# Experts' first layer with the weights as the loaded operand: its rows come out turned, without transposes and copies

## The chip, the cores and the metric

The kernel runs on one core of a Trainium2 chip. The metric is the time of one execution on the device in microseconds (us), smaller being better. The time of before is the median of three runs. Beside it stands one profiled execution, from which all rows come.

## The reference, cut to what matters

Eight images of 64 channels x 128 x 128 go through a normalisation, two 1x1 convolutions and a residual. The pixels then become tokens (16384 per image, 64 values each). Of every image each of 32 experts takes the 8 tokens with the highest gate value, pools them into one row, passes the row through two layers, and adds the result, weighted, back to its 8 tokens:

```
pooled = jnp.einsum('bked,bke->bed', gathered, topv)        # b=8 images, k=8, e=32 experts, d=64
h = jnp.concatenate([pooled.transpose(1, 0, 2), ones], axis=-1)
h = jax.nn.gelu(jnp.einsum('ebd,edh->ebh', h, weight1), approximate=False)   # d=65, h=256
h = jnp.concatenate([h, ones], axis=-1)
out = jnp.einsum('ebh,eho->ebo', h, weight2)                # o=64
outputs = outputs.at[jnp.arange(Bn)[:, None], flat_idx].add(weighted)
```

The change concerns the first of the two expert layers, and the way from it to the second.

## The kernel before

All is written by hand: each engine has its own instruction stream and runs it in order, and semaphores tie the streams together. The eight images go through a pipeline of 8 x 8 steps that fills the first 565 us. Behind it comes a tail in which the experts run, in two passes over the images: `PASSES` is images 0 to 5 (pass 0) and 6 to 7 (pass 1).

The tail's stream on TensorE (PE) is, for pass 0: pool the gathered tokens (`experts_in`, L573), the first layer (`experts_up`, L606), two spreads of a statistic over the partitions for image 7 (`spread_stat` "E", L485), turn the hidden rows (`experts_turn`, L616), one spread for the merge of image 7's candidates ("M", L473), the second layer (`experts_down`, L626), the rows of the outputs (`expert_rows`, L635), and the sums of what is added to the tokens (`add_rows`, L650). Pass 1 is `experts_in`, `experts_up`, `add_rows(1)` (second half of pass 0's sums), `spread_pixels(3)` (L582), `experts_turn`, `experts_down`, `expert_rows`, and two more `add_rows`.

In the first layer the loaded operand of a matmul is the pooled rows (65 values of 32 columns, of which 8 are one expert's images; the others are not used), and the weights stream past it, 256 columns for each expert. Four experts stand side by side in the array, in four groups of 32 columns. The hidden rows come out with (slot of 32, image) on the partitions and the hidden index along the row, in four PSUM banks; ScalarE (ACT) applies the gelu to 128x512 at a time (`gelu`, L835), TensorE transposes 16 blocks of 128x128, and VectorE (DVE) copies the used columns out of PSUM into `ht` (`turned`, L1178). The second layer reads `ht`. Every matmul in float32 stands in the trace as two instructions, each with a weight load of its own; a transpose is one.

DVE's stream in pass 0 goes through the top values and places of image 7 (L963, L968), two scalings of its logits that need the two spreads (`use_spread` "E", L869), the four copies of `turned(0)`, and `candidates(7)` (L975 to L981), whose last instruction waits for ACT's exponentials (L745) and releases the "M" spread.

Of the kernel before, what the change touches and what calls it, by code (L numbers as in the profile page):

```python
# [9 lines left out]
ACT = mybir.ActivationFunctionType  # L10
AX = mybir.AxisListType

P = 128
C = 64
HALVES = 2
NB = 8
PIX = 128 * 128
HW = PIX // HALVES
CH = 512
SUB = 256  # L20
# [5 lines left out]
HID = 256  # L26
# [4 lines left out]
PASSES = ((0, 6), (6, 8))  # L31
# [68 lines left out]
def mk_metaformer_kernel(nc, x, gn_w, gn_b, w1T, b1, w2T, b2, gateT, gate_b, e_w1, e_w2, e_b2, *outs):  # L100
    ctx = ExitStack()
    with ctx:
        def sb(name, shape, dt=F32):
            return ctx.enter_context(nc.sbuf_tensor(name, shape, dt))

        def banks(name, n=1):
            return ctx.enter_context(nc.psum_tensor(name, [P, n * CH], F32))

        def sem(name):
            return ctx.enter_context(nc.semaphore(name))  # L110
# [3 lines left out]
        us = [sb(f"us{i}", [P, HW]) for i in range(2)]  # L114
# [8 lines left out]
        ident = sb("ident", [P, P])  # L123
# [62 lines left out]
        ew1 = us[0][0:C + 1, :].rearrange("d (e n) -> d e n", e=NE)  # L186
        ew2 = xs[0][:, 0:NE * 2 * C].rearrange("p (e k o) -> p e k o", e=NE, k=2)
# [3 lines left out]
        pool_f = late[0:C + 1, 0:NE * NB + 3 * NB]  # L191
        zsq = [eq[:, 6:8].rearrange("p b f i -> p (b f i)"), late[:, CH:2 * CH]]
        diags = [eq[:, 7 - p % 2].rearrange("p f i -> p (f i)") for p in range(3)] + [late[:, 2 * CH:3 * CH]]
        hg = us[1][:, 0:4 * CH]
        ht = us[1][:, 4 * CH:5 * CH]
        eot = us[1][:, 5 * CH:7 * CH]
        zc = us[1][:, 7 * CH:9 * CH].rearrange("p (b g c) -> p b g c", b=NB, g=GATHERS)
# [5 lines left out]
        tl, st1, st2 = banks("tl", 2), banks("st1"), banks("st2")  # L203
        lgp, pt = tl[:, 0:CH], tl[:, CH:2 * CH]
        first_banks = [bc, cv]
        bc_of = [bc[:, 0:CH], bc[:, CH:2 * CH]]
        pc, pd = cv[:, 0:CH], cv[:, CH:2 * CH]
# [1 line left out]
        gnb_p = bc[:, 2:3]  # L209
        mrg_p = bc[:, CH:CH + 4 * MRG]  # L210

        h_banks, add_banks = (st1[:], pt, pd, pc), (lgp, st2[:])


        w_in, x_in = sem("w_in"), [sem(f"x_in{m}") for m in range(NG)]
# [16 lines left out]
        idx_out = sem("idx_out")  # L232
        rows_in = [sem("rows_in0"), sem("rows_in1")]
        scattered = [sem(f"scattered{i}") for i in range(len(outs))]
        zero_ready, ht_ready = sem("zero_ready"), sem("ht_ready")
        t2_done = sem("t2_done")
        ln_steps, rvar_ready, rln_done, ry_ready = (sem(n) for n in ("ln_steps", "rvar_ready", "rln_done", "ry_ready"))
        z_ready, pool_done, pooled_ready = (sem(n) for n in ("z_ready", "pool_done", "pooled_ready"))
        ew_in, l1_done, gelu_done, l2_done = (sem(n) for n in ("ew_in", "l1_done", "gelu_done", "l2_done"))
# [21 lines left out]
        def place(b, i):  # L261

            return PIECE * ((PIECES * b + i) % RING)

        def piece(b, i):
            return lg[:, place(b, i):place(b, i) + PIECE]

        def used(eng, it, kind, k):

            eng.wait_ge(bc_used, job_count(it, kind, k))  # L270
# [86 lines left out]
        def _(pe):  # L357
# [219 lines left out]
            def spread_pixels(p):  # L577

                pe.wait_ge(diag_ready, p + 1)
                pe.wait_ge(bc_used, job_count(7, "L", 1) if p == 0 else job_count(7, "L", 3) if p < 3 else job_count(8, "M", 7))  # L580
                wait(pe, eq_ready, p - 1)
                pe.matmul(bc_of[p % 2], ones[:], diags[p], start=True, stop=True).then_inc(pxr_done, 1)  # L582
# [15 lines left out]
            def experts_up(p):  # L598

                pe.wait_ge(pooled_ready, p + 1)  # L600
                if p == 0:
                    pe.wait_ge(ebias_ready, 1)
                    pe.wait_ge(tok_done, NU * NB)
                for e in range(NE):
                    grp, slot = e // 4, e % 4
                    mm = pe.matmul(h_banks[grp // 2][32 * slot:32 * slot + 32, HID * (grp % 2):HID * (grp % 2) + HID],  # L606
                                   pool_f[:, NB * e:NB * e + 32], ew1[:, e, :], start=True, stop=True, skip_group_check=True)
                    if e % 8 == 7:
                        mm.then_inc(l1_done, 1)

            def experts_turn(p):

                for i in range(4):
                    pe.wait_ge(gelu_done, 4 * p + i + 1)
                    for k in range(4):
                        mm = pe.transpose(h_banks[i][:, P * k:P * k + P], hg[:, CH * i + P * k:CH * i + P * k + P], ident[:])  # L616
                    mm.then_inc(t2_done, 1)

            def experts_down(p):

                pe.wait_ge(ht_ready, 4 * p + 4)
                for e in range(0, NE, 2):
                    for k in range(2):
                        for par in range(2):
                            col = 32 * (2 * (e // 4) + k) + NB * ((e + par) % 4)
                            mm = pe.matmul(pd[C * par:C * par + C, NB * (e // 2):NB * (e // 2) + NB], ew2[:, e + par, k, :],  # L626
                                           ht[:, col:col + NB], start=(k == 0), stop=(k == 1), skip_group_check=True)
                mm.then_inc(l2_done, 1)

            def expert_rows(p):  # L630
# [27 lines left out]
            for h in range(HALVES):  # L658
                mm = pe.matmul(pd[C * h:C * h + C, 0:NE], eb2, ident[0:NE, 0:NE], start=True, stop=True)
# [3 lines left out]
            experts_up(0)  # L663
            for k in (2, 3):
                spread_stat(NB, "E", k)
            experts_turn(0)
            spread_stat(NB, "M", NB - 1)
            experts_down(0)
            expert_rows(0)
# [2 lines left out]
            experts_up(1)  # L672
            add_rows(1)
            spread_pixels(3)
            experts_turn(1)
            experts_down(1)
            expert_rows(1)
            for i in (2, 3):
# [4 lines left out]
        def _(act):  # L683
# [146 lines left out]
            def gelu(p):  # L830

                nc.scalar.preload_act_table_set("gelu_and_others")
                for i in range(4):
                    act.wait_ge(l1_done, 4 * p + i + 1)
                    nc.scalar.activation(hg[:, CH * i:CH * i + CH], h_banks[i], ACT.Gelu).then_inc(gelu_done, 1)  # L835

            gelu(0)
            nc.scalar.preload_act_table_set("natural_log_exp_and_others")
# [8 lines left out]
        def _(dve):  # L847
# [117 lines left out]
            def top_places(t, i):  # L965

                link = Steps(dve, top_steps, TOP_STEPS * t + 2 * i + 1)
                link(nc.vector.max_index(top_i[:, K * i:K * i + K], cnd[:, K * i:K * i + K], piece(t, i)))  # L968
                nc.vector.tensor_scalar(nmax[:, i:i + 1], cnd[:, K * i:K * i + 1], -1.0, None, ALU.mult).then_inc(top_ready, 1)

            def candidates(t):

                link = Steps(dve, top_steps, TOP_STEPS * t + 2 * PIECES)
                pix = cnd[:, CAND:2 * CAND]
                link(nc.vector.tensor_scalar(top_hi[:], top_i[:], 0xFFFFFF00, None, ALU.bitwise_and))  # L975
                link(nc.vector.scalar_tensor_tensor(out=pix, in0=top_i[:], scalar=rowoff[:], in1=top_hi[:],
                                                    op0=ALU.add, op1=ALU.add))
                link(nc.vector.tensor_tensor(pix, pix, pixbase[:], ALU.add))
                assert link.n + 2 * PIECES == TOP_STEPS, link.n
                dve.wait_ge(expl_done, PIECES * (t + 1))  # L980
                nc.vector.tensor_tensor(cnd4[:], cnd[:].unsqueeze(1).broadcast_to([P, 4, MRG]),  # L981
                                        kmask[:].unsqueeze(2).broadcast_to([P, 4, MRG]), ALU.mult).then_inc(cnd4_ready, 1)
# [116 lines left out]
            def equal_pixels(p):  # L1099

                dve.wait_ge(pxr_done, p + 1)
                for i, b in enumerate((2 * p, 2 * p + 1)):
                    for f in range(GATHERS):
                        ins = nc.vector.tensor_scalar(eq[:, b, f, :], bc_of[p % 2][:, SUB * i:SUB * i + SUB],
                                                      px_all[:, b, f:f + 1], None, ALU.is_equal)
                ins.then_inc(eq_ready, 1)
                dve.wait_ge(eq_ready, p + 1)
# [18 lines left out]
            for q in range(4):  # L1126
                r = slice(32 * q, 32 * q + 32)
# [35 lines left out]
            def pooled(p):  # L1163

                b0, b1 = PASSES[p]
                dve.wait_ge(pool_done, p + 1)
                if p == 0:
                    dve.wait_ge(zero_ready, 1)
                else:
                    dve.wait_ge(l1_done, 4)  # L1170
                nc.vector.tensor_copy(pool_f[0:C, 0:NE * NB].rearrange("c (e b) -> c b e", b=NB)[:, b0:b1],
                                      pc[0:C, 0:NE * NB].rearrange("c (b e) -> c b e", b=NB)[:, b0:b1]).then_inc(pooled_ready, 1)

            def turned(p):

                for i in range(4):
                    dve.wait_ge(t2_done, 4 * p + i + 1)
                    nc.vector.tensor_copy(ht[:, P * i:P * i + P].rearrange("p (a b) -> p a b", b=NB),  # L1178
                                          h_banks[i].rearrange("p (a r) -> p a r", r=32)[:, :, 0:NB]).then_inc(ht_ready, 1)

            def expert_outs(p):

# [39 lines left out]
            for i in (2, 3):  # L1222
                top_values(7, i)
                top_places(7, i)
            turned(0)
            candidates(7)
            lns(nc.vector.tensor_tensor(id2[:], ident[:, 0:C], ident[:, C:P], ALU.add))
            use_spread(NB, "M", NB - 1)
# [7 lines left out]
            result_rows(0)  # L1236
            result_rows(1)
            equal_pixels(3)
            turned(1)
            expert_outs(1)  # L1240
            contributions(1)
            for i in (2, 3):
# [101 lines left out]
```

## Time and profile before

| what | value |
|---|---|
| median of three runs | 655.95 us (655.65 to 656.5) |
| profiled execution, its own time | 656.33 us |
| span of the profiled execution | 654.6 us, 14326 instructions |
| busy share of PE / PE weight loads / DVE / ACT / POOL | 84 / 43 / 75 / 66 / 29 % |
| mean granted clock of TensorE | 0.918 |

The profile counts TensorE's matmuls (PE) and its weight loads (PEld) apart. "Granted clock" is the share of full speed: 1.00 is 2.4 GHz, 0.50 is 1.2 GHz. Times are counted from the start of the span.

### The profile page before, as it was taken

How to read it: one execution, taken by the hardware profiler on the slowest of the kernel's cores; microseconds unless marked ns; L12 is line 12 of the kernel's file. 1: busy time of each engine (PE TensorE's matmuls, PEld its weight loads, DVE VectorE, ACT ScalarE, POOL GpSimd, SP SyncE). 2: the span in 40 equal slices, each digit the busy share in tenths (PEclk: the TensorE clock that was granted, in tenths of full speed). 3: DMA queues.
4: the chain of work that ended last, by engine and by line, in shares of the span. 5: the costliest groups of instructions: out<-in, count | busy, mean ns of one | idle time of the engine just before them, and what ended most of it. 6: DMA issues, size and time to landing. Idle time of an engine off the chain costs nothing.

```text
span 654.6 us, 14326 instructions
## 1 busy us (share of the span) xinstructions
PE 547.3 (84%) x5838; PEld 282.9 (43%) x5838; DVE 488.5 (75%) x955; ACT 428.9 (66%) x603; POOL 186.9 (29%) x110
## 2 busy tenths in 40 slices
PE   3659999998989898989898989898979888576983
PEld 1333444444444344435443544354434333346673
DVE  5574565789888988898889888988887779695221
ACT  2454778678967896789678967896779556361200
POOL 1008252116220622062206120612052451101332
PEclk9955999999999999999999999999989989975565
DMA  8950246533653364336533643364111555300000
GB/s 198 198 124 6 85 133 173 154 95 100 182 141 98 106 180 136 101 105 175 139 105 106 177 132 107 111 170 131 67 64 67 159 155 157 109 2 6 12 14 8
DMA packets 26753, 73.40 MB, mean 112 GB/s; under 512 B 4152, under 2 KB 4152, under 8 KB 22592
## 3 DMA queue, kind: packets, MB, share of 16 engines
q1 hardware_dynamic: 25664, 71.44, 39.7%
q0 software_dynamic: 1024, 1.05, 0.6%
q8 instruction: 46, 0.75, 0.5%
q14 instruction: 19, 0.16, 0.1%
HBM read 38.40 MB, written 34.08 MB: 111 GB/s over the span
## 4 chain that ended last, share of the span: by engine, by line
PE 43%; DVE 30%; ACT 13%; issue 11%; DMA 2%; POOL 0%; SPq 0%; ACTq 0%; DVEq 0%; POOLq 0%
PE st L364 11%; ACT junk L740 7%; DVE xs L881 7%; PE cv L375 6%; PE cv L383 6%; PE tl L392 5%; PE bc L485 5%; DVE us L871 4%; DVE lg L869 3%; PE cv L626 2%; DVE top_i L968 2%; ACT tok L705 2%; DVE us L873 2%; PE tl L401 2%; ACT hid L700 2%
## 5 line engine op out<-in xcount | busy, mean ns | idle before, releaser
L1285 POOL TENSOR_TENSOR xs<-xs,us 128x1024 f32<-128x1024 f32 x64 | 151.2, 2380 | 366.3 <-DVE xs L881 173.1
L881 DVE SCALAR_TENSOR_TENSOR xs<-cv,vecs,xs 128x1024 f32<-128x1024 f32 x64 | 82.0, 1282 | 47.7 <-PE cv L383 47.6
L733 ACT ACTIVATE sqc<-us 128x1024 f32<-128x1024 f32 x64 | 67.5, 1054 | 45.4 <-DVE us L871 44.6
L700 ACT ACTIVATE hid<-cv,b1n 128x1024 f32<-128x1024 f32 x64 | 71.3, 1114 | 36.8 <-PE cv L375 36.3
L871 DVE TENSOR_TENSOR us<-xs,bc 128x1024 f32<-128x1024 f32 x60 | 72.9, 1215 | 19.6 <-PE bc L485 19.2
L392 PEld LDWEIGHTS tl<-ident,xs 128*128 128x128 f32 x512 | 63.8, 195 | 53.5 <-issue 53.3
L364 PE MATMUL st<-xs,stat_w 128*32 128x256 f32 x1024 | 74.4, 412 | 10.0 <-DMA xs<-in_x 8.9
L740 ACT ACTIVATE junk<-us 128x1024 bf16<-128x1024 f32 x64 | 67.3, 1051 | 22.8 <-DVE gsum L873 22.2
L873 DVE CUSTOM_DVE_ANT_0 us<-us,bc 128x1024 f32<-128x1024 f32 x60 | 72.9, 1215 | 11.2 <-PE bc L485 9.9
L485 PE MATMUL bc<-rstd_s,spread 32*128 32x256 f32 x368 | 47.7, 336 | 35.6 <-DVE gsum L873 20.3
L392 PE MATMUL tl<-ident,xs 128*128 128x128 f32 x512 | 76.4, 294 | 0.8 <-ACT lg L715 0.8
L375 PE MATMUL cv<-us,w1n 64*64 64x512 f32 x512 | 72.0, 633 | 2.5 <-DVE b1n L936 1.9
L383 PE MATMUL cv<-hid,w2bd 64*64 64x512 f32 x512 | 70.6, 622 | 2.8 <-ACT hid L700 2.8
L401 PE MATMUL tl<-xs,gcen 128*32 128x256 f32 x1024 | 69.4, 389 | 4.0 <-ACT tok L705 4.0
L720 ACT ACTIVATE sqx<-xs 128x1024 f32<-128x1024 f32 x64 | 67.0, 1047 | 1.0 <-PE st L364 0.8
L485 PEld LDWEIGHTS bc<-rstd_s,spread 32*128 32x128 f32 x368 | 28.9, 192 | 86.1 <-DVE gsum L873 42.3
L705 ACT ACTIVATE tok<-tl 128x1024 f32<-128x1024 f32 x64 | 65.0, 1016 | 1.2 <-PE tl L392 1.2
L715 ACT ACTIVATE lg<-tl 128x512 f32<-128x512 f32 x64 | 37.8, 590 | 34.7 <-PE tl L401 31.9
L485 PE MATMUL bc<-mean_s,spread 32*128 32x256 f32 x240 | 31.8, 342 | 19.5 <-DVE us L871 15.1
L364 PEld LDWEIGHTS st<-xs,stat_w 128*32 128x32 f32 x1024 | 31.3, 116 | 33.6 <-issue 13.6
L401 PEld LDWEIGHTS tl<-xs,gcen 128*32 128x32 f32 x1024 | 27.1, 110 | 34.4 <-issue 11.3
L869 DVE TENSOR_TENSOR lg<-lg,bc 128x1024 f32<-128x1024 f32 x32 | 38.9, 1214 | 1.6 <-PE bc L485 1.3
(184 smaller groups left out, 664.6 us busy)
## 6 DMA issues: line engine op xcount, KB each, us to landing
xs<-in_x SPq DMA_DIRECT2D x64, 512.0 KB, 6.8
out_rows<-tok SPq DMA_DIRECT2D x64, 512.0 KB
us<-in_e_w SPq DMA_DIRECT2D x8, 260.0 KB
xs<-in_e_w SPq DMA_DIRECT2D x8, 256.0 KB
sqc<-out_rows,idx_all POOLq DMA_INDIRECT x16
out_rows<-sqc,idx_all POOLq DMA_INDIRECT x16, 2.1
vecs<-in_b SPq DMA_DIRECT2D x4, 0.2 KB, 13.6
gate_bias<-in_gate_b SPq DMA_DIRECT2D x4, 0.1 KB, 11.9
```

The source lines that it names most:

```text
L364: mm = pe.matmul(dst[32 * c:32 * c + 32], stat_w[:, q, :], src[:, col:col + SUB], start=first and m == 0 and sub == 0, stop=True, skip_gro ...
L375: mm = pe.matmul(cv[C * sl:C * sl + C, CH * h:CH * h + CH], w1n[par][r, r], half_chunk(us[par], u, h, sl), start=True, stop=True)
L383: mm = pe.matmul(cv[C * h:C * h + C, CH * sl:CH * sl + CH], w2bd[r, r], hid[r, CH * h:CH * h + CH], start=True, stop=True)
L392: mm = pe.transpose(tl[:, P * k:P * k + P], unit(xs[par], u)[:, k:UN:8], ident[:])
L401: mm = pe.matmul(lgp[NE * c:NE * c + NE, SUB * sl:SUB * sl + SUB], gcen[:, NE * h:NE * h + NE], xs[par][:, col:col + SUB], start=True, sto ...
L485: mm = pe.matmul(out[:, CH * sl + SUB * i:CH * sl + SUB * i + SUB], weights, stat[32 * c:32 * c + 32, :], start=True, stop=True)
L700: nc.scalar.activation(hid[:], cv[:], ACT.Relu, bias=b1n[:, par:par + 1]).then_inc(h_done, 1)
L740: nc.scalar.activation(junk[:], unit(us[n % 2], k), ACT.Square, accum_out=gsq[:, k:k + 1]).then_inc(usq_done, 1)
L871: ins = nc.vector.tensor_tensor(unit(us[n % 2], k), unit(xs[n % 2], k), stat[:], ALU.subtract)
L873: ins = nc.vector.tensor_tensor_reduce(unit(us[n % 2], k), unit(us[n % 2], k), stat[:], 1.0, 0.0, ALU.mult, ALU.add, gsum[:, k:k + 1])
L881: nc.vector.scalar_tensor_tensor(out=xu, in0=cv[:], scalar=vecs[:, 3:4], in1=xu, op0=ALU.add, op1=ALU.add).then_inc(x1_done, 1)
L1285: nc.gpsimd.tensor_tensor(xu, xu, su, ALU.add).then_inc(s_done, 1)
```

## The change

The first layer swaps its operands. For each expert and each half of its 256 hidden values, a 65x128 block of the weights is loaded, and the pooled rows of the pass (6 columns in pass 0, 2 in pass 1) stream past. The hidden values come out on the partitions, which is what the second layer reads; so the transposes on TensorE, the copies on DVE and their two semaphores go. The gelu writes straight into `ht`, in two instructions a pass instead of four. The second layer takes only the pass's columns (6 or 2 instead of 8), and its wait is on the gelu, once for each half of the experts.

```diff
-        h_banks, add_banks = (st1[:], pt, pd, pc), (lgp, st2[:])
+        h_banks, add_banks = (st1, pc), (lgp, st2[:])
...
+        def place_of(e, k):
+
+            return NB * (2 * e + k)
...
+                b0, b1 = PASSES[p]
                 for e in range(NE):
-                    grp, slot = e // 4, e % 4
-                    mm = pe.matmul(h_banks[grp // 2][32 * slot:32 * slot + 32, HID * (grp % 2):HID * (grp % 2) + HID],
-                                   pool_f[:, NB * e:NB * e + 32], ew1[:, e, :], start=True, stop=True, skip_group_check=True)
-                    if e % 8 == 7:
+                    for k in range(2):
+                        col = place_of(e, k)
+                        mm = pe.matmul(h_banks[e // 16][:, col % SUB + b0:col % SUB + b1], ew1[:, e, P * k:P * k + P], pool_f[:, NB * e + b0:NB * e + b1],
+                                       start=True, stop=True)
+                    if e % 16 == 15:
                         mm.then_inc(l1_done, 1)
 
-            def experts_turn(p):
-
-                for i in range(4):
-                    pe.wait_ge(gelu_done, 4 * p + i + 1)
-                    for k in range(4):
-                        mm = pe.transpose(h_banks[i][:, P * k:P * k + P], hg[:, CH * i + P * k:CH * i + P * k + P], ident[:])
-                    mm.then_inc(t2_done, 1)
-
             def experts_down(p):
 
-                pe.wait_ge(ht_ready, 4 * p + 4)
+                b0, b1 = PASSES[p]
                 for e in range(0, NE, 2):
+                    if e % 16 == 0:
+                        pe.wait_ge(gelu_done, 2 * p + e // 16 + 1)
                     for k in range(2):
                         for par in range(2):
-                            col = 32 * (2 * (e // 4) + k) + NB * ((e + par) % 4)
-                            mm = pe.matmul(pd[C * par:C * par + C, NB * (e // 2):NB * (e // 2) + NB], ew2[:, e + par, k, :],
-                                           ht[:, col:col + NB], start=(k == 0), stop=(k == 1), skip_group_check=True)
+                            col, out = place_of(e + par, k), NB * (e // 2)
+                            mm = pe.matmul(pd[C * par:C * par + C, out + b0:out + b1], ew2[:, e + par, k, :],
+                                           ht[:, col + b0:col + b1], start=(k == 0), stop=(k == 1), skip_group_check=True)
...
-            experts_turn(0)
...
-            experts_turn(1)
...
-                for i in range(4):
-                    act.wait_ge(l1_done, 4 * p + i + 1)
-                    nc.scalar.activation(hg[:, CH * i:CH * i + CH], h_banks[i], ACT.Gelu).then_inc(gelu_done, 1)
+                b0, b1 = PASSES[p]
+                for i in range(2):
+                    act.wait_ge(l1_done, 2 * p + i + 1)
+                    half, h = (t.rearrange("p (a b) -> p a b", b=NB)[:, :, b0:b1]
+                               for t in (ht[:, SUB * i:SUB * i + SUB], h_banks[i][:, 0:SUB]))
+                    nc.scalar.activation(half, h, ACT.Gelu).then_inc(gelu_done, 1)
...
-            def turned(p):
-
-                for i in range(4):
-                    dve.wait_ge(t2_done, 4 * p + i + 1)
-                    nc.vector.tensor_copy(ht[:, P * i:P * i + P].rearrange("p (a b) -> p a b", b=NB),
-                                          h_banks[i].rearrange("p (a r) -> p a r", r=32)[:, :, 0:NB]).then_inc(ht_ready, 1)
```

TensorE's stream in pass 0, from the first layer (L606) to the second (L626), before; a row's last figures are the output's shape and the number of matmuls in the source:

```order
L606 MATMUL st<-us,lg 32x256 x8
L606 MATMUL tl<-us,lg 32x256 x8
L606 MATMUL cv<-us,lg 32x256 x16
L485 MATMUL bc<-rstd_s,spread 128x256 x8
L616 MATMUL st<-ident,us 128x128 x4
L616 MATMUL tl<-ident,us 128x128 x4
L616 MATMUL cv<-ident,us 128x128 x8
L473 MATMUL bc<-cnd,fold 128x272
L626 MATMUL cv<-us,xs 64x8 x64
```

The same place now, where the first layer is L610, the spreads are L487 and L475, and the second layer is L624:

```order
L610 MATMUL st<-lg,us 128x6 x32
L610 MATMUL cv<-lg,us 128x6 x32
L487 MATMUL bc<-rstd_s,spread 128x256 x8
L475 MATMUL bc<-cnd,fold 128x272
L624 MATMUL cv<-us,xs 64x6 x64
```

The first layer has 64 matmuls instead of 32, over all 128 columns of the array instead of 32, and it still stands ahead of the two spreads for image 7.

TensorE's stream in pass 1, from the pooling (L573) to the second layer, before:

```order
L573 MATMUL cv<-esel,sqc 64x32 x4
L606 MATMUL st<-us,lg 32x256 x8
L606 MATMUL tl<-us,lg 32x256 x8
L606 MATMUL cv<-us,lg 32x256 x16
L650 MATMUL st<-us,xs 128x64 x12
L582 MATMUL bc<-lg,gsel 128x512
L616 MATMUL st<-ident,us 128x128 x4
L616 MATMUL tl<-ident,us 128x128 x4
L616 MATMUL cv<-ident,us 128x128 x8
L626 MATMUL cv<-us,xs 64x8 x64
```

And now:

```order
L575 MATMUL cv<-esel,sqc 64x32 x4
L610 MATMUL st<-lg,us 128x2 x32
L610 MATMUL cv<-lg,us 128x2 x32
L648 MATMUL st<-us,xs 128x64 x12
L584 MATMUL bc<-lg,gsel 128x512
L624 MATMUL cv<-us,xs 64x2 x64
```

The second layer moves up to directly behind the spread of the pixels (L582, now L584); nothing else has changed places.

DVE's stream in pass 0, around the copies of `turned(0)` (L1178), before; L969 ends the last top places, L981 releases the "M" spread:

```order
L968 MAX_INDEX top_i<-cnd,lg 128x8
L969 TENSOR_SCALAR nmax<-cnd 128x1
L1178 COPY us<-st 128x128
L1178 COPY us<-tl 128x128
L1178 COPY us<-cv 128x128 x2
L975 TENSOR_SCALAR top_hi<-top_i 128x32
L976 SCALAR_TENSOR_TENSOR cnd<-top_i,rowoff,top_hi 128x32
L978 TENSOR_TENSOR cnd<-cnd,pixbase 128x32
L981 TENSOR_TENSOR cnd<-cnd,kmask 128x272
```

Now the four copies are gone from between L969 and L975, and the rest of the stream is as it was.

## Rows read from the trace of the kernel before

**Rows 1.** The page, part 4: shares of the chain that ended last.

```profile
PE 43%; DVE 30%; ACT 13%; issue 11%; DMA 2%; POOL 0%; SPq 0%; ACTq 0%; DVEq 0%; POOLq 0%
```

**Rows 2.** The chain that ended last, pass 0: start us, us, what.

```profile
580.40 1.22 DVE top_i L968 x2
...
581.72 1.23 DVE lg L869
...
583.09 0.53 PE bc L485 x4
...
583.63 1.23 DVE lg L869
...
590.38 0.79 DVE us L1178 x4
...
591.80 0.45 DVE cnd L981
```

**Rows 3.** The same chain, second layer of pass 0 and all of pass 1.

```profile
593.64 7.34 PE cv L626 x128
...
613.20 1.94 PE st L606 x16
...
620.26 5.31 PE st L650 x24
...
630.48 1.34 PE cv L626 x40
...
632.37 1.12 issue
...
633.89 1.03 issue
...
639.39 0.47 DVE us L1189 x4
```

**Rows 4.** Timeline of PE's matmuls: start, us, line, names, columns, form, count.

```profile
576.46 1.82 PE L606 MATMUL st<-us,lg 65*32 65x256 f32 x16
...
580.81 0.51 PE L485 MATMUL bc<-rstd_s,spread 32*128 32x256 f32 x4
...
627.18 1.06 PE L616 MATMUL st<-ident,us 128*128 128x128 f32 x4
```

**Rows 5.** Timeline of PE's weight loads: "128*64" is 128 rows, 64 columns loaded.

```profile
564.58 0.97 PEld L392 LDWEIGHTS tl<-ident,xs 128*128 128x128 f32 x8
...
593.57 6.91 PEld L626 LDWEIGHTS cv<-us,xs 128*64 128x64 f32 x128 [0.70 <-issue]
...
602.60 2.63 PEld L635 LDWEIGHTS tl<-gcen,us 128*128 128x128 f32 x12 [2.12 <-DVE us L1189]
606.47 5.19 PEld L650 LDWEIGHTS tl<-us,xs 128*128 128x128 f32 x24 [1.24 <-DVE us L1199]
```

**Rows 6.** Stretches: length, busy of PE, PEld, DVE, ACT, POOL; PEclk; DMA share; GB/s.

```profile
576.46:578.04 1.58, 1.58 (x20) 0.79 (x16) 1.34 (x2) 1.25 (x4) 0.00 (x0) 0.50 0.00 0
578.04:580.88 2.84, 2.84 (x54) 1.40 (x46) 2.54 (x7) 1.60 (x5) 0.00 (x0) 1.00 0.03 6
...
588.28:591.70 3.42, 0.28 (x2) 0.02 (x1) 3.28 (x11) 1.96 (x4) 0.00 (x0) 1.00 0.00 0
591.70:629.24 37.54, 33.41 (x274) 27.05 (x275) 13.66 (x51) 4.59 (x9) 9.95 (x11) 0.50 0.03 9
629.24:632.66 3.42, 2.50 (x52) 2.12 (x51) 0.94 (x4) 0.00 (x0) 2.66 (x3) 1.00 0.08 29
```

**Rows 7.** Weight loads of two lines: shortest, median, longest in ns; first and last start.

```profile
L626 PEld LDWEIGHTS cv<-us,xs x256: 133/227/231, 593.6 to 639.0; 128*64 128x64 f32 x128
...
L650 PEld LDWEIGHTS tl<-us,xs x32: 288/333/338, 606.5 to 643.5; 128*128 128x128 f32 x32
L392 PEld LDWEIGHTS tl<-ident,xs x512: 185/193/231, 61.1 to 565.4; 128*128 128x128 f32 x171
```

**Rows 8.** Timeline of ACT, the last exponential of image 7.

```profile
590.41 1.15 ACT L745 ACTIVATE lg<-lg,nmax 128x1024 f32<-128x1024 f32 x1 [1.42 <-DVE nmax L969]
...
591.47 0.19 ACT L745 ACTIVATION_READ_ACCUMULATOR lg<-lg,nmax 128x1 f32 x1
```

More of the change, by code:

```diff
@@ L193, in mk_metaformer_kernel @@
         diags = [eq[:, 7 - p % 2].rearrange("p f i -> p (f i)") for p in range(3)] + [late[:, 2 * CH:3 * CH]]
-        hg = us[1][:, 0:4 * CH]
         ht = us[1][:, 4 * CH:5 * CH]
@@ L234, in mk_metaformer_kernel @@
         scattered = [sem(f"scattered{i}") for i in range(len(outs))]
-        zero_ready, ht_ready = sem("zero_ready"), sem("ht_ready")
-        t2_done = sem("t2_done")
+        zero_ready = sem("zero_ready")
         ln_steps, rvar_ready, rln_done, ry_ready = (sem(n) for n in ("ln_steps", "rvar_ready", "rln_done", "ry_ready"))
@@ L1169, in pooled @@
                 else:
-                    dve.wait_ge(l1_done, 4)
+                    dve.wait_ge(l1_done, 2)
                 nc.vector.tensor_copy(pool_f[0:C, 0:NE * NB].rearrange("c (e b) -> c b e", b=NB)[:, b0:b1],
                                       pc[0:C, 0:NE * NB].rearrange("c (b e) -> c b e", b=NB)[:, b0:b1]).then_inc(pooled_ready, 1)
-            def turned(p):
-                for i in range(4):
-                    dve.wait_ge(t2_done, 4 * p + i + 1)
-                    nc.vector.tensor_copy(ht[:, P * i:P * i + P].rearrange("p (a b) -> p a b", b=NB),
-                                          h_banks[i].rearrange("p (a r) -> p a r", r=32)[:, :, 0:NB]).then_inc(ht_ready, 1)
             def expert_outs(p):
@@ L1224, in _ @@
                 top_places(7, i)
-            turned(0)
             candidates(7)
@@ L1238, in _ @@
             equal_pixels(3)
-            turned(1)
             expert_outs(1)
```

## The prediction

> **What bounds the kernel now.** I read the page first, for the chain that ended last: 43% of it is TensorE and 30% VectorE [rows 1], so no one engine bounds the whole. The change touches only the tail, so I read the chain there, in order of time. In pass 0 it does not run through the first layer: it runs through DVE, from the top places of image 7 over the two scalings L869 to the candidates L981 [rows 2]. The first layer of pass 0 is beside it, from 576.46 to the start of the spread at 580.81 [rows 4], and DVE is busy with L968 until just ahead of 581.72 [rows 2]. But the spread that the first scaling needs stands behind the first layer in TensorE's stream, and it starts less than 1 us before DVE asks for it. That layer has almost no slack. From 593.64 on the chain is TensorE and what it hands to DVE and gets back: second layer, sums, then in pass 1 the first layer itself (613.20 to 620.26), the sums, the transposes, and the second layer from 630.48 to 639.39 [rows 3]. What pass 1 gains or loses counts in full.
>
> Next I read the weight loads and the clock, since the change trades long streams for loads. What the reader is to see is what sets the pace where the streamed part is short. L650 loads 128 columns and streams 64: 24 loads in 5.19 us, one lasting 0.333 us, so (5.19 - 0.333) / 23 = 0.211 us from one to the next [rows 5, 7]. L635, the same shape, gives (2.63 - 0.333) / 11 = 0.209 [rows 5]. L626 loads 64 columns and streams 8, two matmuls side by side: (6.91 - 0.227) / 63 = 0.106 us a pair [rows 5, 7]. It streams an eighth of the columns and takes half the time: the pace follows the loaded columns, not the streamed ones. The load of 128 columns lasts 333 ns and that of 64 lasts 227, which is 106 ns for 64 columns [rows 7], the same slope. All of these stand in the stretch from 591.70 to 629.24 where the granted clock is 0.50 (1.2 GHz) [rows 6]. At clock 1.00, L392 has (0.97 - 0.193) / 7 = 0.111 us from one 128-column load to the next [rows 5, 7].
>
> **The first layer, new.** 64 matmuls in float32 are 128 instructions, each with its own load of 128 columns over the whole width of the array, so no two stand side by side. With 6 or 2 columns streamed, the load sets the pace: 128 x 0.213 us = 27.3 us at the low clock, 128 x 0.111 = 14.2 us at the high one. I take 0.213, a little over the 0.209 and 0.211 of the loads, in which the first is short; the top is L650's 5.31 us on the chain over its 24 instructions, 0.221, which holds the drain of the last one too [rows 3]. The nearest row streams 64 columns and not 6. Below, the bound is a cost by streamed columns alone: L626's 7.34 / 128 = 0.057 us an instruction [rows 3]. I take the high end, since L626 with 8 columns follows it too.
>
> The Trainium skill's page "TensorE: Matmul & The Clock Gate", section "LDWEIGHTS (loading the stationary operand)", puts a load at the loaded columns divided by 1.2, in ns, whatever the number of rows: 107 ns for 128 columns. The trace agrees at the high clock (0.111) and shows twice that at the low one (0.211). By the page's figure the two passes would cost 27.4 us together instead of some 53.
>
> **Which clock.** The kernel before had 0.50 until 578.04, with TensorE streaming 256-column matmuls without a break, and 1.00 after [rows 6]. Now such streams end at 576.46. The second layer and the sums, both bound by loads, kept TensorE busy 33.41 of 37.54 us and the clock stayed at 0.50 [rows 6]. It rose at 629.24 behind a 512-column matmul and transposes, and fell again at 632.66, with the load-bound second layer running since 630.48 [rows 3, 6]. The short high stretches are 3.42 us long [rows 6]. So pass 1's first layer runs at the low clock throughout, and pass 0's at best gets such a stretch near its start: it would fit 3.42 / 0.111 = 31 instructions instead of 16, a saving of 15 x 0.213 = 3.2 us. Whether it comes I can't read off; I take half, 1.6 us. All low and two such stretches are the bounds.
>
> **Pass 0, step by step.** Start 576.46, end 576.46 + 27.3 - 1.6 = 602.2. Then the first spread: 0.53 us at the high clock [rows 2], at most twice that at the low one, say 0.8; DVE's first L869 starts at 603.0 instead of 581.72: **+21.3**. The second spread lies on the chain as well and is slower by the same: +0.25. Behind it DVE's work is as before. The four copies (0.79 us on the chain, 590.38) look like a gain, but L981 also waits for ACT's last exponential, which ends at 591.47 + 0.19 = 591.66, and L981 started at 591.80 [rows 2, 8]: the gain is **-0.1**. If that cover were gone, it would be 0.8. The transposes of pass 0 lie beside DVE's chain and give nothing; nor does the shorter gelu. The "M" spread and the second layer (64-column loads, low clock) stay as they are: 8 columns or 6 is nothing against the load. All of POOL's gathers and adds move along. Pass 0: +21.3 + 0.25 - 0.1 = **+21.45**.
>
> **Pass 1.** The first layer: 27.3 instead of 620.26 - 613.20 = 7.06 [rows 3]: **+20.25**, in full, since the sums of `add_rows(1)` wait behind it in the stream. The transposes and copies: from 627.18, where the first matmul of L616 started [rows 4], to 630.48, the second layer [rows 3]: **-3.3**. The gelu is done long before, since 24 instructions of L650 and the pixels' spread lie between. The second layer took 639.39 - 630.48 = 8.91 us, with issue gaps of 1.12 and 1.03 us (and one of 0.24) in it, at a stretch where it ran partly at the high clock; in pass 0, all at the low clock, it took 7.34 without a gap [rows 3]. Now it has no transposes ahead of it, so I give it 7.4: **-1.5**. The bounds are 0 (gaps stay) and -1.6. Pass 1: +20.25 - 3.3 - 1.5 = **+15.45**.
>
> **Sum.** +21.45 + 15.45 = +36.9 us. The profiled execution's own time is 656.33: 693.2. It is 0.4 over the median of the runs, so I forecast **692.8 us**, against 655.95.
>
> **Rivals.**
> - *The loads take about 0.11 us each at any clock, or the clock is high all through* (the page's figure, as above). Pass 0 ends at 576.46 + 14.2 = 590.7, DVE's L869 at 591.4, +9.7 - 0.1; pass 1 is 14.2 - 7.06 - 4.8 = +2.3. Sum +11.9: 667.9. Against it stand 24 loads at 0.211 us. Chance 0.05.
> - *The clock rises at 578.04 as before and stays until pass 0's first layer is over.* 1.58 us at the low clock fit 7 instructions, the other 121 take 13.4 us: end 591.4 instead of 602.2, so 692.8 - 10.8 = 682.0. For it: the clock did rise there and the time from 578.04 to 580.88 was all high [rows 6]. Against it: the fall at 632.66, in the middle of load-bound work. Chance 0.05.
> - *The other side: the first layer costs by what it streams.* If a load hid behind its neighbour, 6 and 2 columns would cost like L626's instructions, 0.057 us: 7.3 us a pass. Pass 0 then ends 2.9 us later than the 4.4 that are free (+2.9 + 0.25 - 0.1), pass 1 is 7.3 - 7.06 - 4.8 = -4.6. Sum -1.5: 654.4. It decides at 4.4 + 7.06 + 4.65 = 16.1 us for both passes, 0.063 us an instruction. For it: pass 1's first layer streams 256 columns in 0.44 us and its 32-column loads add nothing that shows. Against it: L650's loads are not hidden, with 64 columns to hide behind. Chance 0.03.
> - *The forecast*, load-bound at the low clock: 0.87.
>
> **How the numbers follow.** Within the forecast: no high stretch gives +1.6, a pace of 0.216 instead of 0.213 +0.8, the streamed columns, if they add to the load, +1.7 (pass 1's first layer now has 64 instructions in 7.06 us, four abreast: 0.44 us for 256 columns, so 10 ns for 6 and 3 ns for 2, times 128 each), the gaps of the second layer kept +1.5; together 5.6: 698. Two high stretches give -4.7 and a pace of 0.209 -1.0: 687. Own range 687 to 698. The clock's rival lies at 682 and the page's at 668; a range of 685 to 699 leaves less than 2 in 10 out. Differences below 0.2% (1.3 us) can't be told from none. Faster 0.02, same 0.01, slower 0.97.
>
> **What the profile would show.** The first layer as 128 weight loads of 65x128 at 0.21 us in each pass; the second L869 pair starting at 603 and 605; L981 at about 613; the granted clock at 0.50 from about 580 to the end, if for one short stretch; pass 1's first layer of 27 us on the chain, and the second layer directly behind L582's successor, without gaps. I'd be wrong if loads of 65 rows went faster than those of 128, if a load could run during another matmul's short stream, or if these loads kept the clock high.

## The result and the profile after

The changed kernel takes 697.16 us (median of 4 runs, 696.13 to 698.94), against 655.81 us of the kernel before on the same chips: a ratio of 1.0625, 95% interval 1.0611 to 1.064. It is slower by 41 us. Its profiled execution has a time of 696.13 us and a span of 694.4, 39.8 us more than before on both counts. Medians, ratios and intervals below leave out an execution that took over 1.5% longer than the fastest of its kernel: one of four of `w64` (683.2 us) and one of ten of `before_late` (1596.6 us).

From the page of the changed kernel, the slices and the shares of the chain:

```profile
PE   3569988989898989898989889998888869759983
...
PEclk9757999999999999999999999999999985555555
...
PE 47%; DVE 27%; ACT 13%; issue 10%; DMA 1%; another core or an unknown queue 0%; POOL 0%; SPq 0%; ACTq 0%; DVEq 0%; POOLq 0%
```

TensorE's share of the chain (the last line) rises from 43% [rows 1] to 47%, and the last slices show TensorE busy at half the clock. The chain itself, in order of time (start, us, what), in pass 0:

```profile
577.09 10.64 PE st L610 x64
587.73 13.65 PE cv L610 x64
601.38 0.75 PE bc L487 x4
...
602.15 1.23 DVE lg L868
...
604.35 1.23 DVE lg L868
...
611.13 1.25 ACT lg L741 x2
...
612.47 0.46 DVE cnd L980
...
614.31 7.31 PE cv L624 x128
```

The first layer (L610) is now on the chain in pass 0, where it had been beside it. DVE's first scaling (L868, before L869) starts at 602.15 instead of 581.72, the candidates at 612.47 instead of 591.80 [rows 2], and the second layer at 614.31 instead of 593.64 [rows 3]. Each is 20.4 to 20.7 us late: nothing of the loss is given back between them. The copies that went give nothing, and the row of ACT shows why: the last exponential (L741) starts at 611.13 and ends at 612.38, just ahead of 612.47.

A small part of this is not the change's: the first layer itself starts at 577.09, where it started at 576.46 before [rows 4], behind the same instructions. Other executions reach this place between 574.7 (`w32`) and 580.9 (`w64`), so a start-to-start distance within the tail says more than the total of one execution.

The same chain in pass 1:

```profile
633.85 13.81 PE st L610 x64
647.66 13.65 PE cv L610 x64
661.32 5.22 PE st L648 x24
...
668.35 3.77 PE cv L624 x65
672.12 0.95 issue
673.07 0.39 PE cv L624 x4
...
675.97 3.15 PE cv L624 x54
...
679.22 0.47 DVE us L1181 x4
```

The first layer lasts from 633.85 to 661.32, 27.47 us, where it was 7.06 [rows 3]. The way from its end to the second layer is 7.03 us (661.32 to 668.35) instead of 10.22, without the transposes. The second layer takes 10.87 us (668.35 to 679.22) instead of 8.91, with issue gaps in it.

The first layer's loads (shortest, median, longest in ns) and three stretches (length; busy of PE, PEld, DVE, ACT, POOL; granted clock; DMA share; GB/s):

```profile
L610 PEld LDWEIGHTS cv<-lg,us x128: 333/333/333, 587.5 to 660.9; 65*128 65x128 f32 x128
```

```profile
577.01:580.10 3.09, 3.09 (x32) 3.09 (x28) 2.59 (x6) 2.85 (x7) 0.00 (x0) 0.98 0.00 0
580.10:601.30 21.20, 21.20 (x103) 21.19 (x102) 2.02 (x5) 2.86 (x4) 0.00 (x0) 0.51 0.00 1
...
633.85:661.30 27.45, 27.45 (x129) 27.45 (x129) 0.36 (x1) 0.23 (x1) 5.84 (x6) 0.50 0.02 8
```

A load of 65x128 lasts 333 ns, as the 128x128 loads of before at the low clock did [rows 7]. PE and PEld are busy all the time (21.20 and 21.19 of 21.20 us in pass 0, 27.45 of 27.45 in pass 1), and yet the clock goes down to 0.50 three microseconds into pass 0's layer and does not come back. 27.45 us for 128 instructions is 0.2145 us each; the 3.09 us at clock 0.98 passed 28 loads, 0.110 each.

### The profile page after: what moved, and what is told of

It is laid out like the page before. It is cut to its first block, busy times and chain, and to the rows that moved or that the text cites. A ratio compares the mean times of both kernels' runs of the same rounds, so it can differ in the third digit from the quotient of the medians.

```text
span 694.4 us, 14506 instructions
## 1 busy us (share of the span) xinstructions
PE 584.9 (84%) x5934; PEld 324.7 (47%) x5934; DVE 486.8 (70%) x947; ACT 425.6 (61%) x599; POOL 186.6 (27%) x110
## 3 DMA queue, kind: packets, MB, share of 16 engines
q0 software_dynamic: 1024, 1.05, 0.5%
## 4 chain that ended last, share of the span: by engine, by line
PE 47%; DVE 27%; ACT 13%; issue 10%; DMA 1%; another core or an unknown queue 0%; POOL 0%; SPq 0%; ACTq 0%; DVEq 0%; POOLq 0%
PE st L366 10%; ACT junk L736 6%; DVE xs L880 6%; PE cv L377 6%; PE cv L385 5%; PE tl L394 5%; PE bc L487 5%; DVE us L870 5%; PE cv L610 4%; PE st L610 4%; DVE lg L868 3%; PE cv L624 2%; ACT tok L701 2%; DVE us L872 2%; DVE top_i L967 2%
## 5 line engine op out<-in xcount | busy, mean ns | idle before, releaser
L487 PE MATMUL bc<-rstd_s,spread 32*128 32x256 f32 x368 | 48.4, 341 | 33.6 <-DVE gsum L872 20.3
L487 PEld LDWEIGHTS bc<-rstd_s,spread 32*128 32x128 f32 x368 | 29.4, 195 | 84.9 <-DVE gsum L872 42.3
L868 DVE TENSOR_TENSOR lg<-lg,bc 128x1024 f32<-128x1024 f32 x32 | 38.9, 1214 | 21.8 <-PE bc L487 21.5
L487 PE MATMUL bc<-mean_s,spread 32*128 32x256 f32 x240 | 31.6, 340 | 19.7 <-DVE us L870 15.1
## 6 DMA issues: line engine op xcount, KB each, us to landing
vecs<-in_b SPq DMA_DIRECT2D x4, 0.2 KB, 13.8
gate_bias<-in_gate_b SPq DMA_DIRECT2D x4, 0.1 KB, 12.2
```

The costliest lines, as they stand in the source:

```text
L487: mm = pe.matmul(out[:, CH * sl + SUB * i:CH * sl + SUB * i + SUB], weights, stat[32 * c:32 * c + 32, :], start=True, stop=True)
```

## The experiments

Each was run beside the kernel before on the same chip. In the tables of lines, the first layer is L610 or L611, the second L624 or L626.

**More columns streamed (`n32`).**

```diff
-    mm = pe.matmul(h_banks[e // 16][:, col % SUB + b0:col % SUB + b1], ew1[:, e, P * k:P * k + P], pool_f[:, NB * e + b0:NB * e + b1], ...)
+    mm = pe.matmul(h_banks[e // 16][:, col % SUB:col % SUB + 32], ew1[:, e, P * k:P * k + P], pool_f[:, NB * e:NB * e + 32], ...)
```

> The changed kernel, but its first layer streams 32 columns for each load (as many as before the change) instead of 6 or 2; the surplus columns are overwritten or not read. If the load of 128 columns sets the pace alone, each pass's first layer keeps its time (27.5 us in pass 1, 0.2135 us an instruction) and the total stays at 697 within 2 us. Rival, the streamed columns add to the load: 1.7 ns a column, so 26 more columns in pass 0 cost 128 x 0.045 = 5.7 us and 30 more in pass 1 cost 6.6 us, 709 in all.

Measured: 698.2 us, ratio 1.0623 (1.0595 to 1.0652), the same as the changed kernel. Pass 1's first layer in the timeline of TensorE, and what follows it:

```profile
636.70 13.86 PE L610 MATMUL st<-lg,us 65*128 65x32 f32 x64 [0.36 <-DVE lg L1170]
650.38 13.84 PE L610 MATMUL cv<-lg,us 65*128 65x32 f32 x64
664.03 5.36 PE L648 MATMUL st<-us,xs 128*128 128x64 f32 x24
```

From 636.70 to 664.03 is 27.33 us, and with 2 columns the same two starts lie 27.33 us apart (633.85 and 661.18). Thirty more columns cost nothing: what is streamed, up to 32 columns, does not set the pace. (In pass 0 this execution got no high stretch of the clock, and its first layer took 27.5 us instead of 24.3.)

**Narrower loads (`w64`, `w32`).** The same products, with each block of 128 columns loaded in pieces that go to different column groups of the array:

```diff
-    mm = pe.matmul(h_banks[e // 16][:, ...], ew1[:, e, P * k:P * k + P], pool_f[:, NB * e + b0:NB * e + b1], ...)
+    for j in range(0, P, 64):        # 32 in w32
+        mm = pe.matmul(h_banks[e // 16][j:j + 64, ...], ew1[:, e, P * k + j:P * k + j + 64], pool_f[:, NB * e + b0:NB * e + b1], ...)
```

> The changed kernel with each 65x128 block loaded as two blocks of 65x64, side by side in the array: 256 instructions a pass instead of 128. Theory (load time is by loaded columns, and two column groups load side by side): a pair every 0.107 us at the low clock, so 13.7 us a pass instead of 24.3 and 27.5; total 697.2 - 10.6 - 13.7 = 673. Rival (one load at a time in the whole array): 256 x 0.107 = 27.3 us a pass, total unchanged at 697.

> The changed kernel with each block loaded as four of 65x32, four abreast: 512 matmul instructions a pass. Theory: four every 0.053 us at the low clock, 6.8 us a pass, total 697.2 - 17.5 - 20.6 = 659. Rival (loads side by side cost what one does only until the instructions' own issue binds; the starts of instructions in one group lie 7 ns apart, and a group would be 8 instructions with its loads): 56 ns or more a group, up to 9 us a pass, 660 to 664. If loads are serial, 697.

Measured: 675.6 us with pieces of 64 (672.75 to 679.88; ratio 1.0273, 1.0243 to 1.0303) and 676.1 with pieces of 32 (1.0306, 1.0288 to 1.0323). Pass 0's first layer in the run with 64:

```profile
580.94 7.00 PE L611 MATMUL st<-lg,us 65*64 65x6 f32 x128
587.79 6.98 PE L611 MATMUL cv<-lg,us 65*64 65x6 f32 x128
```

It takes 13.8 us where 128-column loads took 27.5 at the low clock: twice the instructions in half the time, since two groups load side by side. Theory and price hold for pass 0. In pass 1 the same layer took 18.0 us, with gaps, beside POOL's scatters: 4.3 us over what I had put, where the median is 2.6 over the 673 that I had expected. The profiled execution is the one of 679.88; it had reached the first layer at 580.94, 3.9 us later than the changed kernel's. Pieces of 32 come to a new limit. Two rows of its pass 0 and two of its pass 1:

```profile
581.92 1.89 PE L611 MATMUL cv<-lg,us 65*32 65x6 f32 x128 [1.56 <-issue]
585.38 1.15 PE L611 MATMUL cv<-lg,us 65*32 65x6 f32 x71 [1.56 <-issue]
...
620.86 0.29 PE L611 MATMUL st<-lg,us 65*32 65x2 f32 x6 [0.44 <-issue]
...
628.05 2.19 PE L611 MATMUL st<-lg,us 65*32 65x2 f32 x149 [1.14 <-issue]
```

In pass 0, 128 matmuls (and as many loads) run in 1.89 us and then TensorE stands for 1.56 us with nothing to wait for. In pass 1, while POOL scatters, it gets 4 to 6 matmuls at a time with gaps of 0.44 to 1.15 us. The expected 6.8 us a pass became 11.75 and 20.5: neither the arrays nor the data bound this version. What is left is how fast TensorE gets its instructions, and for the long gaps the trace has rows on that. The DMA queues from the start of a burst to the next one (`w32`, 581.92 to 585.38; the first row has what moved, in 40 equal slices):

```profile
GB/s 0 0 0 0 0 0 0 0 0 0 0 0 189 0 0 0 0 0 0 0 0 0 0 0 0 0 0 0 0 0 0 0 0 0 0 0 0 0 0 0
DMA packets 1, 0.02 MB, mean 5 GB/s; under 512 B 0, under 2 KB 0, under 8 KB 0
...
q8 instruction: 1, 0.02, 1.7%
```

One packet of 16 KB moves, on the queue called instruction, from 583.03 for 0.94 us, and TensorE resumes 1.4 us after its end. The burst from 581.92 was 256 instructions (128 matmuls, 128 loads). The whole trace has 53 such packets here and 47 in the changed kernel, and TensorE has 1536 instructions more, which is 6 x 256. Each of the 12 long gaps in and right behind the first layers of `w32` and `w32_hold` ends 1.35 to 1.57 us after the end of such a packet. In pass 0 of `w32` the packets start 3.43 to 3.51 us apart (576.09, 579.60, 583.03, 586.50), so TensorE gets 256 instructions in some 3.5 us and runs them in 1.89.

**The scatters out of the way (`late`).**

```diff
+                if (b, g) == (3, 0):
+                    pool.wait_ge(l2_done, 2)
```

> The changed kernel, but POOL's last six scatters of images 3 to 5 wait until pass 1's second layer is done, instead of running beside it. Pass 1's second layer took 10.9 us with five issue gaps of 2.8 us in all, where pass 0's took 7.3 without one. Theory A (the gaps come from the scatters running beside it): 7.3 us and no gaps; the six scatters of 1.27 us each then come at the end and give back up to 2 us, total 694 to 696. Theory B (the gaps have to do with TensorE's own instruction supply at this place): the gaps stay, and the total is 697 to 700.

Measured: 694.8 us, ratio 1.0583 (1.0565 to 1.06). The second layer of pass 1 in TensorE's timeline, and the first held scatter in POOL's:

```profile
669.80 7.00 PE L624 MATMUL cv<-us,xs 128*64 128x2 f32 x128
```

```profile
677.59 0.97 POOL L1299 DMA_INDIRECT out_rows<-sqc,idx_all  x1 [34.19 <-PE cv L624]
```

All 128 in one piece, in 7.00 us. In the changed kernel the scatters stood here, by its timeline of POOL:

```profile
667.40 0.96 POOL L1297 DMA_INDIRECT out_rows<-sqc,idx_all  x1 [25.55 <-DVE sqc L1200]
...
673.76 0.97 POOL L1297 DMA_INDIRECT out_rows<-sqc,idx_all  x1 [0.30 <-issue]
```

They ran from 667.40 to 674.7 and the layer's gaps lie between 672.1 and 676.0. Theory A holds. The held scatters then bind the end: from the layer's start to the end of the last scatter it is 20.5 us (669.88 to 690.39) instead of 21.7 (668.35 to 690.06), so about 2.7 us of the 3.9 are given back there.

These gaps are not those of `w32`'s pass 0. The only queue with packets between 668.35 and 675.97 of the changed kernel is that of the scatters:

```profile
q0 software_dynamic: 192, 0.20, 7.2%
```

No instruction packet moves there, and TensorE gets one to four matmuls at a time and resumes 0.71 to 0.75 us after the last time (673.07, 673.82, 674.53, 675.25, 675.97).

**The same in the kernel before (`before_late`, `before_late3`).** `before_late` has the edit above; `before_late3` holds only the last three of the six, with `(3, 1)` in place of `(3, 0)`.

> The kernel before, with the last six scatters of images 3 to 5 held back until pass 1's second layer is done, and nothing else. Theory A (scatters starve TensorE of instructions, whatever the clock): the second layer of pass 1 takes 7.0 us or less instead of 8.9, without issue gaps; the scatters, 1.27 us each, then bind the end, which costs up to 2.7 us: total 655 to 658. Theory B (gaps come with the high clock, as the prediction had it): the gaps stay, 8.9 us.

> The kernel before, with only the last three of the six scatters held until pass 1's second layer is done; the first three, 626.4 to 630.2 in its trace, are over before that layer starts. Theory (scatters beside the second layer starve it): 4 to 7 us for the layer instead of 8.9 without gaps, by the clock that it gets; the three scatters left (3.8 us) fit ahead of the last ones, so that the end is bound by the chain again: 652 to 655. Rival (no gain beyond the noise, since the chain's end moves to POOL anyway): 656.

Measured: 654.7 us, ratio 0.996 (0.994 to 0.998), and 652.2 us, ratio 0.9931 (0.9908 to 0.9954). The second layer of pass 1 in each:

```profile
632.52 3.90 PE L626 MATMUL cv<-us,xs 128*64 128x8 f32 x128 [0.62 <-DVE us L1178]
```

```profile
630.67 5.22 PE L626 MATMUL cv<-us,xs 128*64 128x8 f32 x128 [0.38 <-DVE us L1178]
```

Without scatters beside it there is no gap at the full clock (1.00 in the first stretch, 3.90 us) nor at a mixed one (0.71 in the second, 5.22 us). And the changed kernel has gaps, beside scatters, at 0.50. So it is the scatters that make the gaps of [rows 3], not the clock. Of the kernel before's six, the fourth and the sixth, from its timeline of POOL:

```profile
630.26 0.97 POOL L1307 DMA_INDIRECT out_rows<-sqc,idx_all  x1 [0.30 <-issue]
...
632.82 0.97 POOL L1307 DMA_INDIRECT out_rows<-sqc,idx_all  x1 [0.31 <-issue]
```

Its second layer starts at 630.48: three scatters were over by then, and three were not. Holding those three is enough, and costs less at the end than holding six. `before_late3` is faster than the kernel before, by 0.7%, and so than the changed one.

**The spreads ahead of the first layer (`efirst`, `efirst_act`).**

```diff
-            experts_up(0)
             for k in (2, 3):
                 spread_stat(NB, "E", k)
+            experts_up(0)
```

> The changed kernel with the two spreads for image 7 ahead of pass 0's first layer in TensorE's stream. Theory (in pass 0 the cost is that DVE's two scalings wait behind the 128 loads): DVE's chain then runs as in the kernel before, its candidates are done near 592, and what waits instead is the M spread behind the first layer. That starts at about 584.0, the spreads being done, and ends 27.3 us later at 611.3, so the M spread comes at 611.3 instead of 613 to 616: total 697.2 - 2.8 = 694.4, between 692 and 697. Rival (the loads are bound elsewhere, DVE's wait is not what counts): unchanged within 1 us. The bigger point is what it can't do: 27 us don't fit beside a DVE chain of 9 us.

Measured: 699.0 us, ratio 1.0637 (1.0603 to 1.0671): no gain, and outside what I had expected. The chain between the two layers:

```profile
597.08 13.67 PE cv L610 x64
...
610.77 0.34 ACT us L834
...
611.13 1.28 ACT L837
612.42 2.38 ACT lg L741 x4
...
614.90 0.45 DVE cnd L980
...
615.49 1.25 PE bc L475 x2
```

DVE's chain did run ahead, as expected. But the candidates (L980) wait for two exponentials (L741), and in ACT's stream these stand behind the gelu, which waits for the end of the first layer, and a change of tables. I had moved the wait to the queue of an engine that I had not looked at. `efirst_act` puts the two exponentials ahead of the gelu:

```diff
+            for i in (2, 3):
+                explog(7, i)
             gelu(0)
             nc.scalar.preload_act_table_set("natural_log_exp_and_others")
-            for i in (2, 3):
-                explog(7, i)
```

> The kernel with the two spreads first, and now also ACT's last two exponentials of image 7 ahead of pass 0's gelu. With the spreads first alone the M spread came at 615.5 and not at 611.3: ACT's stream held the second half of the gelu (waiting for the first layer's end at 610.75) ahead of the exponentials for which the candidates wait, 4.6 us with the change of tables. Theory: the M spread now comes directly behind the first layer, near 611, and the total is 699.0 - 4.5 = 694.5. Rival (something else holds the candidates): unchanged at 699.

Measured: 695.5 us, ratio 1.0582 (1.0566 to 1.0599). The chain there:

```profile
599.05 13.65 PE cv L610 x64
612.71 1.11 PE bc L475 x2
```

The M spread follows on the first layer with nothing between. Only now is pass 0, from the layer's start behind the spreads (585.30) on, bound by the loads alone, and the kernel gains 1.6 us over the changed one by the medians (0.4% by the ratios): a layer of 27 us does not fit beside a DVE chain of 11 (581.7 to 592.4 in the kernel before), in whatever order.

**Both together (`w64_hold`, `w32_hold`).** Narrow loads, the spreads first, the last six scatters as in `late`, and the first six held until pass 1's first layer is done:

```diff
+                if (b, g) == (0, 0):
+                    pool.wait_ge(l1_done, 4)
```

> The changed kernel, loads split in two 65x64 side by side, the two spreads ahead of pass 0's first layer, the first six scatters held until pass 1's first layer is done and the next six until its second layer is done. Theory: pass 0's first layer from 584.0 to 597.8, M spread at 597.8 (5.4 later than in the kernel before); pass 1's first layer 13.9 us without gaps instead of 18.0 in the run with split loads alone (6.8 more than before); transposes -3.3, second layer -1.5, end +2.7 for the scatters: 656.2 + 10.1 = 666. If the gaps are not the scatters' doing: 670.

> The same with the loads split in four 65x32. With 512 matmul instructions and as many loads the supply of instructions should bind: bursts of 128 in 1.89 us with 1.56 us between, 11.75 us a first layer, as pass 0 had it with split loads alone. Pass 0: 584.0 to 595.8, M spread 3.4 later than in the kernel before; pass 1: 11.75 instead of 7.06 is +4.7; transposes -3.3, second layer -1.5, end +2.7: 656.2 + 6.0 = 662. If the short gaps beside the scatters stay, 670.

Measured: 672.35 us (ratio 1.0222, 1.0191 to 1.0254) and 669.85 us (1.0185, 1.0147 to 1.0223). Pass 1's first layer with pieces of 64, from the timeline:

```profile
624.83 7.00 PE L611 MATMUL st<-lg,us 65*64 65x2 f32 x128 [0.36 <-DVE lg L1172]
631.68 6.97 PE L611 MATMUL cv<-lg,us 65*64 65x2 f32 x128
```

and the end of the one with pieces of 32:

```profile
628.59 1.88 PE L611 MATMUL cv<-lg,us 65*32 65x2 f32 x128 [1.23 <-issue]
632.32 1.89 PE L611 MATMUL cv<-lg,us 65*32 65x2 f32 x127 [1.85 <-issue]
```

The step that I wanted to see is there: the layer of 64s takes 13.8 us instead of 18.0, and the short gaps of the 32s are gone while the long ones stay (12.2 us instead of 20.5), as they should if only the long ones wait for instruction packets. Both totals are 6 to 8 us over what I had expected. Most of that is the ACT queue of `efirst`, which I did not know of when I wrote them down: with 64s the first layer of pass 0 ends at 599.3 and the M spread starts at 604.05, 4.8 us later. With 64s nearly all the rest is that the layer starts at 585.5, not at the 584.0 that I had put; with 32s it starts at 586.1. Neither version comes down to the kernel before.

## Why the prediction was right, and where a term was off

The forecast was 692.8 us, in a range of 685 to 699; the median is 697.2. The mechanism held, and each term can be read off the chain.

- **The pace.** 0.213 us a load was predicted and 0.2145 is measured over pass 1's layer (128 in 27.45 us). `n32` shows that the streamed columns do not count, `w64` that the number of columns loaded one behind the other does. This was argued from rows that stream 64 and 8 columns and is now shown for 2, 6 and 32. A matmul occupies the same columns of the array as its load, so `w64` alone does not tell the two apart; that a load lasts 333 ns for 128 columns and 227 for 64 points at the load. The rival that prices by streamed columns is out.
- **The clock.** 0.50 in pass 1's layer throughout. In pass 0's it was near full for the first 3.1 us, so the profiled execution took 24.3 us instead of my 25.7, which had half of such a stretch; `n32`, `late` and `efirst` did not get it. The rivals with a high clock (667.9 and 682.0) are out. The ground for the forecast was weaker than I wrote: the 37.54 us at 0.50 that I put down to the second layer and the sums also hold pass 1's old first layer, 7 us of 256-column streams.
- **Pass 0.** +20.67 us at the M spread (613.06 by the timeline, 592.39 before), against +21.45. Of this 0.55 us was there when the layer started (577.01 by the timeline, 576.46 before); the layer itself gave +19.9. The copies gave about 0.05 us: from the second scaling to the candidates it is 8.12 us now and was 8.17. The exponential covers them, as predicted. Which stream waits for which is shown by `efirst` and `efirst_act`, one of which corrected me on ACT's part.
- **Pass 1, the first layer.** +20.41 against +20.25.
- **Pass 1, the transposes.** -3.19 (7.03 instead of 10.22) against -3.3.
- **Pass 1, the second layer: the term that was off.** I had given it 7.4 us, so -1.5, with the sentence "now it has no transposes ahead of it", and taken the gaps to come with the high clock. It took 10.87 us, +1.96. The gaps come from POOL's scatters: `late` has 7.00 us without one, `before_late` has none at the full clock. In the changed kernel the scatters start at 667.40 and the layer at 668.35, so five of the six start beside it, up to 674.7; before, three of the six were over when it began. Taking the transposes out had moved the layer under the scatters: it starts 0.95 us after the first of them, not 4.04. This is 3.5 us. My bound for this term reached only to 0.

The sum of the four, 20.65 up to the start of pass 1's layer, +20.41, -3.19 and +1.96, is 39.83, and the two spans differ by 39.8. Against my own terms that is -0.78, +0.16, +0.11 and +3.46: the profiled execution came out 2.9 us over my 693.2. The median lies another 1.0 over it, and I had taken 0.4 off.

That the time lies inside the range is in part luck. The range had room for a missing high stretch and for gaps kept, but not for 3.5 us of new ones. The profiled execution got its high stretch whole; without it, the 28 loads that ran in it would have cost some 28 x (0.2145 - 0.110) = 2.9 us more (my estimate), and 699.0 is the very end of the range.

What stays open is by what path a scatter holds up TensorE. The gaps are put down to "issue", and they fall away with the scatters, in `late`, `before_late`, `before_late3` and both versions with held scatters. They do not wait for the 16 KB packets of `w32`'s long gaps: in the changed kernel none moves between 659.4 and 676.9. Beside pass 1's first layer, which needs only 256 instructions (matmuls and loads) in 27 us, the first six scatters (634.49 to 641.9) make no gap at all.

The Trainium skill's page "TensorE: Matmul & The Clock Gate", section "LDWEIGHTS (loading the stationary operand)", has 107 ns for 128 columns whatever the rows. The rows don't count here either (a load of 65 rows lasts 333 ns like one of 128), and from one load to the next the high stretch agrees (0.110 us). At the low clock, where this kernel's tail runs, the measured pace is twice that.

## What to carry to other kernels

Which operand to load is a question of the columns loaded one behind the other and of the clock, not only of transposes saved: a float32 product with 2 or 6 columns to stream pays 0.21 us for each full-width load at the low clock, and the 16 transposes of 128x128 and their copies saved here were worth 3.2 us in pass 1 and nothing in pass 0. Before moving a wait, read every queue on the way of what is waited for; here ACT's order undid what TensorE's order had won. Where issue gaps stand in a dense run of small instructions, look at what POOL sends at that time: holding three scatters back by 6 us made the kernel before 0.7% faster.

## What the hardware showed that I had not expected

- Full-width loads back to back keep PE and PEld busy all the time, 21.2 us in pass 0 and 27.45 in pass 1, and the granted clock stays at 0.50 or goes down to it.
- Issue gaps beside indirect scatters: 0.36 to 0.95 us each in a layer that needs 256 instructions (loads and matmuls) in 7 us, with no instruction packet moving meanwhile; none without scatters, even at 3.9 us for the same 256.
- With 1024 instructions in a layer, TensorE's supply breaks without any scatter: 128 matmuls with their loads in 1.89 us, then 1.56 us of nothing, again and again. One 16 KB packet moves for every 256 instructions, and in pass 0 of `w32` one started every 3.43 to 3.51 us; the layer that took 3.9 us for its 256 had no gap.
